# Other fill lists for the start, the first and the last batch of a gated cross-attention and feed-forward kernel

## The reference

```
q = (layernorm(x) @ Wq.T) * 32**-0.5         # 16 heads of 32
k = ctx @ Wk.T ;  v = ctx @ Wv.T
o = sigmoid(q k^T) v                         # per head; no softmax
x1 = x + tanh(g_xattn) * (o @ Wo.T)
h = gelu(layernorm(x1) as 8 experts x 448 tokens @ w1 + b1)   # 512 -> 2048
out = x1 + tanh(g_ffn) * (h @ w2 + b2)                        # 2048 -> 512
```

## Time and profile before

| | |
|---|---|
| median of three runs | 1755.41 us |
| the profiled execution, its own time | 1752.19 us |
| its span, first to last instruction | 1750.4 us |
| TensorE busy | 1710.4 us, 98% of the span |
| ScalarE busy | 777.1 us, 44% |
| VectorE busy | 708.5 us, 40% |
| GpSimd busy | 209.3 us, 12% |
| granted TensorE clock, mean | 0.994 of 2.4 GHz |
| 16 DMA engines, mean | 174 GB/s, 305.41 MB |
| TensorE's work from 45 to 1080 us | no wait but small ones: 2.7 and 1.8 us in all |

### The profile page before, as it was taken

One profiled execution on the slowest core, in us unless ns is written; L12 is line 12 of the kernel. 1 busy time (PEld: TensorE's weight loads), 2 busy tenths in 40 slices (PEclk: granted clock), 3 DMA queues, 4 the chain that ended last, 5 costly groups with the idle time before them and its releaser, 6 DMA issues.

```text
span 1750.4 us, 34541 instructions
## 1 busy us (share of the span) xinstructions
PE 1710.4 (98%) x12560; PEld 1513.9 (86%) x12560; DVE 708.5 (40%) x1328; ACT 777.1 (44%) x1020; POOL 209.3 (12%) x301
## 2 busy tenths in 40 slices
PE   6999999999999999999999999799999999999999
PEld 5888888888888888888888887699999999999998
DVE  4323323323333333233233232356555464655553
ACT  4545545446445455455454454433343333333332
POOL 1112212212111111122122121000000000000000
PEclk9999999999999999999999999899999999999999
DMA  7767667667577567576775776354353635445251
GB/s 237 199 174 210 187 190 202 176 190 211 163 200 211 165 197 206 167 210 189 184 212 170 193 204 190 117 183 143 124 186 104 213 107 186 131 136 172 94 186 58
DMA packets 193132, 305.41 MB, mean 174 GB/s; under 512 B 24624, under 2 KB 148048, under 8 KB 192976
## 3 DMA queue, kind: packets, MB, share of 16 engines
q1 hardware_dynamic: 169696, 225.73, 45.5%
q0 software_dynamic: 23280, 77.64, 12.7%
HBM read 224.74 MB, written 78.54 MB: 173 GB/s over the span
## 4 chain that ended last, share of the span: by engine, by line
PE 96%; DMA 1%; DVE 1%; ACT 1%; issue 1%; SPq 0%; POOLq 0%; DVEq 0%; ACTq 0%
PE fill_ps L494 41%; PE scores_ps L654 18%; PE fill_ps L635 13%; PE scores_ps L526 10%; PE heads_ps L540 9%; PE heads_ps L635 4%; PE fill_ps L554 1%; DMA k_scr<-k_stage 1%; DVE k_stage L898 0%; ACT k_stage L717 0%; PE scores_ps L494 0%; SPq L287 0%; DMA probs<-WKT_in 0%; PE fill_ps L590 0%; DMA xnT<-stat_scr 0%
## 5 line engine op out<-in xcount | busy, mean ns | idle before, releaser
L692 ACT ACTIVATE probs<-scores_ps 125x1792 f32<-125x1792 f32 x192 | 319.9, 1666 | 119.0 <-PE heads_ps L540 69.2
L494 PE MATMUL fill_ps<-ctx_hl,wK 128*128 128x250 f32 x2304 | 313.5, 286 | 20.1 <-DVE k_stage L898 9.8
L494 PEld LDWEIGHTS fill_ps<-ctx_hl,wK 128*128 128x128 f32 x2304 | 287.4, 193 | 42.8 <-issue 30.2
L654 PE MATMUL scores_ps<-ctx_hl,wK 128*128 128x448 f32 x1536 | 316.7, 362 | 0.4 <-ACT st_row L723 0.4
L654 PEld LDWEIGHTS scores_ps<-ctx_hl,wK 128*128 128x128 f32 x1536 | 288.0, 188 | 20.5 <-issue 0.7
L494 PE MATMUL fill_ps<-wV,ctx_hl 128*125 128x512 f32 x1152 | 286.4, 398 | 1.3 <-DVE wV L847 1.3
L494 PEld LDWEIGHTS fill_ps<-wV,ctx_hl 128*125 128x125 f32 x1152 | 208.3, 186 | 51.0 <-issue 1.6
L635 PE MATMUL fill_ps<-wQ,wV 128*128 128x448 f32 x1152 | 244.2, 367 | 0.0
L454 POOL DMA_DIRECT2D k_scr<-k_stage x192 | 139.9, 729 | 828.9 <-DVE k_stage L898 807.1
L635 PEld LDWEIGHTS fill_ps<-wQ,wV 128*128 128x128 f32 x1152 | 217.3, 189 | 17.0
L526 PE MATMUL scores_ps<-q_st,k_st 96*125 96x224 f32 x1536 | 203.1, 275 | 8.2 <-DMA q_st<-q_scr 4.5
(11 more groups left out here) (77 smaller groups left out, 1367.9 us busy)
## 6 DMA issues: line engine op xcount, KB each, us to landing
k_st<-k_scr SPq DMA_DIRECT2D x576, 125.0 KB, 3.0
v_sb<-w_in SPq DMA_DIRECT2D x96, 512.0 KB, 4.4
k_scr<-k_stage POOLq DMA_DIRECT2D x192, 250.0 KB, 4.0
ctx_raw<-ctxT_in SPq DMA_DIRECT2D x48, 500.0 KB, 5.0
q_st<-q_scr SPq DMA_DIRECT2D x192, 112.0 KB, 3.4
k_stage<-w_in SPq DMA_DIRECT2D x32, 512.0 KB, 3.6
q_scr<-q_stage POOLq DMA_DIRECT2D x64, 224.0 KB, 3.8
x_ln<-x_in SPq DMA_DIRECT2D x16, 448.0 KB, 4.9
```

Source lines behind the costliest of these rows:

```text
L494: last = pe.matmul(out_, lhsT(kt, a), rhs(kt, c), start=(kt == 0 and t == 0), stop=(kt == KT - 1 and t == 2))
L654: last = pe.matmul(y_ps[:, dt, 0:T], w2[:, slot, a, k, dt * P:(dt + 1) * P], hid_hl[:, slot, d, k, :], start=(c == 0 and k == 0 and t == 0 ...
L692: nc.scalar.activation(probs[0:ST, s % 3], scores_ps[0:ST, :, 0:2 * L], ACT.Sigmoid, scale=SCALE).then_inc(s_probs, 1)
```

## The change

The list for the middle batches moves one fill: S goes from step 6 (after U) to step 7 (after Q 0). The prologue, the first and the last batch get lists of their own:

```
     FILL = [...
-            (6, "U", 1), (6, "S", 0), (7, "K", 7), (7, "Q", 0), (7, "V", 0), ...
+            (6, "U", 1), (7, "K", 7), (7, "Q", 0), (7, "S", 0), (7, "V", 0), ...
-    FILL_FIRST = [(0, "K", 8), (1, "K", 11), (2, "V", 0), (3, "V", 1), (4, "K", 9), (5, "V", 2), (6, "T", 0), (6, "T", 1),
-                  (7, "K", 10), (8, "Q", 0), (9, "Q", 1), (10, "V", 3)]
+    FILL_FIRST = [(0, "K", 8), (1, "K", 11), (2, "T", 0), (2, "T", 1), (3, "Q", 0), (4, "Q", 1), (5, "V", 0), (6, "V", 1),
+                  (7, "K", 9), (8, "K", 10)]
+    FILL_0 = [f for f in FILL if f[1] in "KQTV" and f[1:] not in (("V", 4), ("V", 5))]
+    FILL_0 += [(0, "V", 6), (1, "V", 7), (2, "V", 4), (2, "V", 5)]
+    FILL_LAST = [f for f in FILL if f[1] == "O" or f[1:] in OWN]
+    FILL_LAST += [(2, "Q", 3), (4, "U", 0), (5, "U", 1), (9, "S", 0)]
-    BANK_BESIDE = {("K", 5): 2, ("K", 6): 2, ("K", 7): 2, ("U", 0): 2, ("U", 1): 2, ("S", 0): 2}
+    BANK_BESIDE = {(k, i): g % 3 for g, (_, k, i) in enumerate(FILL_LAST)} | {("K", 6): 0, ("K", 7): 2, ("S", 0): 2}
-    W_SPLITS = {0: (2, 3), 4: (4,), 6: (5,), 9: (6,), 10: (7,)}
-    CTX_FIRST = {1: 1, 5: 2}
+    W_HI = {2: (4,), 3: (5,), 7: (6,), 8: (7,)}
+    W_LO = {1: (2,), 2: (3, 4), 3: (5,), 7: (6,), 8: (7,)}
+    CTX_HI = {5: 2}
+    CTX_LO = {4: 1, 5: 2}
-    HIDDEN_AT = {7: (0, 0), 8: (0, 1), 11: (1, 0)}
+    HIDDEN_AT = {8: (0, 0), 10: (0, 1), 11: (1, 0)}
```

V 6 and V 7 are the value tiles 2 and 3 of the first batch, computed in its own steps 0 and 1 (`tile_of`). The weights are split and loaded in the order K, Q, V, O, x comes ahead of the second context chunk, and the first layernorm is put ahead of the prologue's steps:

```
@@ SyncE
-                    if known(b, B - 1) and s == 2:
+                    if known(b, B - 1) and s == 1:
                         expert_start()
+                    if known(b, B - 1) and s == 3:
+                        load_norm(0)
                     if known(b, B - 1) and s == 5:
-                        load_norm(0)
-                    if known(b, B - 1) and s == 6:
                         load_w1(0, 2)
...
+                    if known(b, B - 1) and s == 5:
+                        gather_q(b, 3)
...
-            load_ctx(0, 0, 0, 1)
+            load_x(x_ln[0:LT], 0, s_x_in)
             load_w(2)
             load_w(3)
-            load_x(x_ln[0:LT], 0, s_x_in)
+            load_ctx(0, 0, 0, 1)
@@ TensorE, fill: queries of the prologue start when half of the query weights is split (values likewise)
-                    if known(b, -1):
-                        pe.wait_ge(s_w_lo, 6)
+                    if known(b, -1) and i == 0:
+                        first = {"halves": 2}
@@ ScalarE
-            w_hi(0)
-            w_hi(1)
+            for n in range(4):
+                w_hi(n)
+            ctx_hi(0, 0, 0, 1)
@@ VectorE
+                    ln_at = (7, 8) if known(b, B - 1) else (3, 4)
-                    if follows(b) and s in (3, 4):
-                        ln_x1(b, 0 if s == 3 else 1)
+                    if follows(b) and s in ln_at:
+                        ln_x1(b, ln_at.index(s))
...
+                        if s == 3:
+                            e_lo(0, 1, 0)
                         if s == 4:
-                            e_lo(0, 1, 0)
-                        if s == 5:
                             normalise(0)
...
+            ln_x(0, 0, 1, 2)
             batches(dve, body)
```

More of the change, by code:

```diff
@@ L61, in flamingo_block @@
             (3, "K", 3), (4, "K", 4), (4, "Q", 3), (5, "K", 5), (5, "T", 0), (5, "T", 1), (6, "K", 6), (6, "U", 0),
[1 row of a table removed]
[1 row of a table added]
             (10, "K", 10), (10, "Q", 1), (10, "V", 2), (11, "K", 11), (11, "V", 3)]
-    FILL_FIRST = [(0, "K", 8), (1, "K", 11), (2, "V", 0), (3, "V", 1), (4, "K", 9), (5, "V", 2), (6, "T", 0), (6, "T", 1),
-                  (7, "K", 10), (8, "Q", 0), (9, "Q", 1), (10, "V", 3)]
+    OWN = [("K", i) for i in range(8)] + [("V", 4), ("V", 5), ("Q", 2)]
+    FILL_FIRST = [(0, "K", 8), (1, "K", 11), (2, "T", 0), (2, "T", 1), (3, "Q", 0), (4, "Q", 1), (5, "V", 0), (6, "V", 1),
[4 more added lines that the diff above has]
+    FILL_LAST += [(2, "Q", 3), (4, "U", 0), (5, "U", 1), (9, "S", 0)]
+    FILL_0.sort(key=lambda f: f[0])
+    FILL_LAST.sort(key=lambda f: f[0])
     K_FIRST = {8: 1, 11: 2, 9: 3, 10: 4}
@@ L86, in fills @@
         if known(b, 0):
-            return [f for f in FILL if f[1] not in "OUS"]
+            return FILL_0
         if known(b, B - 1):
-            return [f for f in FILL if f[1] == "O" or f[1:] in OWN] + [(10, "U", 0), (10, "U", 1), (10, "S", 0)]
+            return FILL_LAST
         if known(b, B):
@@ L97, in bank_of @@
     def bank_of(b, kind, i):
-        if known(b, B - 1) and (kind, i) in BANK_BESIDE:
+        if known(b, 0):
+            return BANK_0[kind, i]
+        if known(b, B - 1):
             return BANK_BESIDE[kind, i]
@@ L324, in body @@
                     for kind, i in fills_at(b, s):
-                        if kind == "Q":
+                        if kind == "Q" and not (known(b, B - 1) and i == 3):
                             gather_q(b, i)
+                    if known(b, B - 1) and s == 5:
+                        gather_q(b, 3)
             def load_xt(e):
@@ L490, in three_terms @@
                 for kt in range(KT):
-                    if halves and kt % (KT // 2) == 0:
-                        pe.wait_ge(halves, 2 * kt // KT + 1)
+                    if halves is not None and kt % (KT // 2) == 0:
+                        pe.wait_ge(s_w_lo, halves + 2 * kt // KT + 1)
                     for t, (a, c) in enumerate(TERMS):
@@ L560, in fill @@
                     if known(b, -1) and i == 8:
-                        first = {"halves": s_w_lo}
+                        first = {"halves": 0}
                     last = three_terms(ps[:, 0:SC], lambda kt, a: w["K"][:, a, kt, mt * P:(mt + 1) * P],
@@ L565, in fill @@
                 elif kind == "V":
-                    c, r = i // 2, i % 2
+                    c, r = tile_of(i) // 2, i % 2
+                    first = {}
                     if r == 0:
@@ L569, in fill @@
                     if known(b, -1) and i == 0:
-                        pe.wait_ge(s_w_lo, 4)
+                        first = {"halves": 4}
                     last = three_terms(ps[0:ST, :], lambda kt, a: ctx_hl[:, c, a, kt, r * ST:(r + 1) * ST],
-                                       lambda kt, a: w["V"][:, a, kt, :])
+                                       lambda kt, a: w["V"][:, a, kt, :], **first)
                 elif kind == "Q":
@@ L739, in leave_v @@
                     act.wait_ge(s_w_lo, 2 * len(w))
-                nc.scalar.copy(v_sb[0:ST, place, i, :], fill_bank(b, "V", i)[0:ST, :]).then_inc(done["V"], 1)
+                nc.scalar.copy(v_sb[0:ST, place, tile_of(i), :], fill_bank(b, "V", i)[0:ST, :]).then_inc(done["V"], 1)
             def body(b, h, par):
@@ L756, in body @@
                     if known(b, -1):
[L757 removed]
+                        for n in W_HI.get(s, ()):
                             w_hi(n)
[L759 to L760 removed]
+                        if s in CTX_HI:
+                            ctx_hi(0, 0, 0, CTX_HI[s])
                         if s == 11:
```

28 lines of the change are left out of this document (13 added, 15 removed), and 2 rows, old and new, of the table FILL.

## The result

| | before | after |
|---|---|---|
| median | 1754.88 us (4 runs) | 1738.59 us (4 runs, 1737.11 to 1741.90) |
| ratio, 95% interval | | 0.9907 [0.9894, 0.9920] |
| profiled execution, span | 1752.19, 1750.4 | 1737.11, 1735.4 |
| granted TensorE clock, mean | 0.994 | 0.997 |

The spans of the two profiled executions differ by 15.0 where the sum said 17.9: the last batch gives less than it was priced at. Measured once more (e10_after_again), the same two kernels stood at 0.9868 [0.9842, 0.9893], 22 us apart, so a measurement can be off by more than its interval says.

A forecast was written before the change was run, and what follows sets the result against it. TensorE, busy 1710.4 of 1750.4 us, was taken as the bound, leaving idle time and low-clock stretches to win. Terms -2.9, 0 and -15.0 sum to -17.9: 1752.2 to 1734.3, plus 3.2 to the median, 1737.5; range 1732 to 1745.

The forecast's parts named there:

- The start: Prologue and first batch: first scores at 31.6 instead of 40.22, step 3's at 53.2 instead of 56.1; gain 2.9 us.
- Rival 3: Start: scores still begin where K 9 and the queries let them, gain 0, 1740.4 us; counted within the forecast's 0.72.
- S: Fourteen batches, S one step later: its wait moves to V 0, which waits for K 7; gain 0.
- +1.4 end of the whole: Slow end for moving S in 14 batches: the handing over costs 0.1 us more each time.
- Rival 4: Fourteen batches: K 7 leaves late and V 0 waits, 1.8 us each giving 1759.7 us, slower; chance 0.03.
- Rival 2: Start gives 5 us and S's wait truly goes, V 0 not waiting: 1731.6 us; chance 0.12.
- The last batch: Last batch: earlier loads and norms remove K 7's 9.8 us wait; heads at 1109.2 instead of 1124.89; 15.0 us taken.
- the clock's 0.7: Last batch: charge for the 1.8 us wait perhaps pulling the clock down once, taking the gain from 15.7 to 15.0.
- 0.1 and 0.35 in steps 9 and 10: Last batch: small TensorE waits still expected in these two steps, part of 3.15 us of remaining waits.
- the 1.8: Last batch, step 8: expected 1.8 us wait for step 7's sigmoid, standing behind the two copies of the tokens.
- The rule on the function table: ScalarE ahead of gelu: the skill's drain of about 1.38 us would make the sum 1.0 smaller; the trace was followed.
- Rival 1: Last batch: norms still late behind K 2's gather and its store, stall at K 6 stays, 1743.6 us; chance 0.13.

The follow-up runs named there:

- e10_after_again: The changed kernel, unaltered, measured again on the same chip as the kernel before: 1737.51 us, 0.9868 of the kernel before.
- e3_start_only: The changed kernel with S back in step 6 and the old last batch, so only the start is new: 0.9980 of the kernel before.
- e6_k9_first: The changed kernel with K 9 between the prologue's two value tiles and the output weights' splits of step 8 together: 0.9896 of the kernel before.
- e12_best_w1_late: The changed kernel with S behind V 0, K 9 earlier, Q 3's gather first, and a quarter of the expert's weights requested behind K 5's gather: 1728.44 us, 0.9836 of before.
- e5_s_after_v: The changed kernel with S one place further, behind V 0 in step 7 of the middle batches: 1730.93 us, 0.9858 of the kernel before.
- e9_s_v_k9: The changed kernel with S behind V 0 and K 9 earlier in the prologue, together: 1734.09 us, 0.9849 of the kernel before.
- e1_s_only: The kernel before with only S moved to step 7 of the middle batches: 0.9998 of the kernel before.
- e2_last_only: The kernel before with only the last batch's new list, loads and orders; start and S as before: 0.9920 of the kernel before.
- e11_best: The changed kernel with S behind V 0, K 9 earlier in the prologue and Q 3's gather first in the last batch: 1733.71 us, 0.9849 of before.

## Why the prediction was right or wrong

**The start: right in mechanism and place, its exact size luck.** -2.9 was forecast and -2.86 measured; 31.6 and 53.2 were the marks, 31.71 and 53.25 came. The bank wait was 0.74 for 0.9, the wait for K 9 0.81 for 1.3, and the clock fell through the queries as the layout had it. e3_start_only has the new start alone: its step 3 stands at 54.99, which is 2.9 and 4.1 ahead of the two kernels with the old start measured with it. But the mark moves by 2.6 us between executions with the new start and by 3.0 with the old one, so an agreement within 0.1 is chance; what the runs show is a gain of 1.1 to 6.7, with 2.9 well inside. Rival 3, no gain at the start, is out by that, and by the interval of e3_start_only only just (0.9993 at its end). The choice that carried the term was to take the low clock's price from rows of before; in e6_k9_first that stretch was 0.9 shorter.

**S: right.** The sum had 0 and said that the wait moves to V 0. It did: 13 waits ahead of V 0 show in the 14 batches, of 0.29 on the mean where 0.1 to 0.2 was said; the batch grew by 0.08, inside the +1.4 end of the whole. The step that was short is the handing over: V 0 begins 0.13 behind K 7's leaving, and the layout had 0.05 (211.84 and 211.89). Rival 4 had the right mechanism, at a fifth of the wait from which it would have decided. Rival 2 was wrong on S.

**The last batch: the mechanism right, the term mis-sized.** -15.0 was forecast and 12.2 measured in the profiled execution. There is no wait ahead of K 7, no idle time ahead of `normalise`, and 1.51 for the sigmoid where 1.8 was said. The work and the waits from 3b to H were laid out as 34.6 with the clock's 0.7, and took 37.40. The term that failed is "0.1 and 0.35 in steps 9 and 10": the scores of step 9 waited 1.96 for the gather of Q 3. The low clock then lay behind that wait and not behind the 1.8, and cost 1.5 on the heads and 0.2 on the scores instead of the 0.7 charged; the waits of steps 5 to 8 were 0.8 below their terms. That makes 36.3; the other 1.1 are small gaps beyond the 0.6 laid out. The layout followed the norms, K 2, K 5's leaving and the banks, but not what stands behind K 5's gather in SyncE's list, although the rival on the norms was built on just such a queue. In e12_best_w1_late, with that gather first, the stretch takes 34.05, which is the laid out 34.6 within 0.6. How much the omission costs depends on the execution: the six with this last batch took 35.17 to 41.02, 37.4 on the mean, so one of them could have stood 0.5 beside the layout and another 6.4, with the same step missing.

**What the forecast of 1737.5 owes to luck.** The profiled executions differ by 15.0 and the medians by 16.3; the sum was 17.9. The offset of 3.2 from the profiled run to the median of before was kept, and the median after lies 1.5 above its profiled run. The errors go opposite ways: 2.8 too much gain (17.9 for the 15.1 between the two executions' own times), 1.7 too much offset. The 1.1 that is left is luck, and so is that the profiled execution had the short feed-forward, as the one before had: e10_after_again, the same kernel, had the long one, 5.5 us more.

**The rule on the function table.** It was weighed against the trace and left out of the sum. ScalarE after, ahead of the first gelu:

```profile
1109.37 1.28 ACT L839 ACT_TABLE_LOAD   x1
1110.67 1.16 ACT L839 ACTIVATE x_ln<-fill_ps,b_sb 128x448 f32<-128x448 f32 x2
```

The load takes 1.28 again, begins 0.02 after the sigmoid ahead of it has ended, and gelu begins 0.02 behind it. The room up to the copy of the last heads is 0.61, where it was 1.45. The drain of about 1.38 us that the Trainium skill ("ScalarE: Activation LUTs", What ACT_TABLE_LOAD costs) adds to a change of set is in neither trace.

**Rival 1** was the right kind of rival: a load that stands behind a gather that waits for a store. It named the norms; it was the query.

## What to carry to other kernels

When a stall is removed by asking for data earlier, lay out the whole list of the queue that asks, to its last transfer before the next wait, and not only the transfer that was late: a request whose data have long been ready still waits for the one ahead of it. Here that was a wait of 0.9 to 3.95 us. A fill's price depends on the bank it inherits: moving a small matmul by one place changed which fill waits for which, and the place next to the scores cost 0.03 us where the one ahead of a large fill cost 0.57. Idle time of 1.5 to 2.4 us on TensorE is to be priced twice, once alone and once with the work behind it at half pace, since both came here. And before a gain of a few us is believed, see how far the same stretch moves between executions of the same kernel.

## What the runs showed of the hardware

- The lower clock followed waits of TensorE of 1.96 (after), 2.54 (e5_s_after_v), 2.82 (e10_after_again) and 3.95 us (e9_s_v_k9): 3.97 to 4.71 for the 48 matmuls behind them instead of 2.48. The length of the wait alone doesn't decide it. Waits of 2.10 (e9_s_v_k9) and 2.31 (e1_s_only) at the loop's turn were followed by heads of 2.48, and one of 1.57 (e2_last_only) by heads of 4.06. The wait of 1.51 or 1.52 in step 8 was followed by full clock in nine executions, and in e11_best by a tile of 4.17.
- The turn of TensorE's loop cost between 0.6 and 5.6 us, and differs between executions with the same instructions.
- The feed-forward of one and the same kernel took 625.5 or 631.0 us, with 365 or 368 ns a matmul in its hidden tiles. It kept its pace to the end, at a granted clock of 1.00 both times: from 1300 to 1500 us TensorE did 994 matmuls after and 985 in e10_after_again, from 1500 to 1700 us 995 and 985. What sets the pace stays open.
